# Two-layer cross-attention on one core: the layer-1 unit's second LayerNorm pass, its gamma pass and its beta pass move later in the turn

## What is computed

```python
def layer(emb, latent, Wq, bq, Wk, bk, Wv, bv, gamma, beta):
    q = emb @ Wq + bq                       # 224 x 512
    k = latent @ Wk + bk                    # 750 x 512
    v = latent @ Wv + bv
    w = softmax((q @ k.T) / sqrt(512), axis=query rows)
    x = w @ v + emb
    mu, var = mean(x, -1), var(x, -1)
    return (x - mu) * rsqrt(var + 1e-6) * gamma + beta
out = layer(layer(x, ctx, L0 weights), ctx, L1 weights)
```

## Time and profile before

| | us |
|---|---|
| median of 3 runs | 1000.95 (1000.65 to 1000.99) |
| the profiled execution, its own time | 1000.18 |
| its span, first to last instruction | 998.4 |
| TensorE busy | 975.7 (98%) |
| VectorE busy | 859.5 (86%) |
| ScalarE busy | 760.2 (76%) |
| GpSimd busy | 766.1 (77%) |
| TensorE's granted clock, mean | 0.998 of full speed |

### The profile page before, as it was taken

How to read it: one execution, slowest core, us unless ns; L and a number is a source line. 1 busy time by engine, 2 the same in 40 slices (tenths; PEclk the granted TensorE clock), 3 DMA queues, 4 the chain that set the end, 5 groups by cost and what they waited for, 6 DMA issues and landing times.

```text
span 998.4 us, 25754 instructions
## 1 busy us (share of the span) xinstructions
PE 975.7 (98%) x7300; PEld 910.6 (91%) x7300; DVE 859.5 (86%) x2602; ACT 760.2 (76%) x2128; POOL 766.1 (77%) x709
## 2 busy tenths in 40 slices
PE   7999999999999999999999999999999999999997
PEld 6889999999999999999999999999999999999986
DVE  5888988988888988888888888898888898888867
ACT  3667887777887777887777787777788777788764
POOL 0437788887888787878778878787878878888884
PEclk9999999999999999999999999999999999999999
DMA  7754443554344454343455344455444455434101
GB/s 207 178 104 103 98 102 89 106 116 98 82 101 97 95 112 99 82 104 94 93 112 104 83 99 100 86 112 106 85 99 97 86 112 111 94 91 103 37 17 50
DMA packets 358998, 98.37 MB, mean 99 GB/s; under 512 B 308648, under 2 KB 342821, under 8 KB 358949
## 3 DMA queue, kind: packets, MB, share of 16 engines
q1 hardware_dynamic: 356405, 96.98, 43.8%
q10 hardware_dynamic: 2544, 0.80, 0.4%
HBM read 83.06 MB, written 14.68 MB: 98 GB/s over the span
## 4 chain that ended last, share of the span: by engine, by line
PE 90%; DVE 3%; SPq 2%; issue 2%; ACT 1%; POOL 1%; DMA 1%; DVEq 0%; ACTq 0%; POOLq 0%
PE oq_bank L787 9%; PE score_bank L743 9%; PE score_bank L748 8%; PE score_bank L744 8%; PE oq_bank L797 6%; PE pv_bank L834 6%; PE oq_bank L772 6%; PE pv_bank L836 6%; PE pv_bank L843 6%; PE oq_bank L720 5%; PE oq_bank L715 5%; PE oq_bank L716 5%; PE oq_bank L773 5%; PE t_bank L672 2%; PE oq_bank L810 1%
## 5 line engine op out<-in xcount | busy, mean ns | idle before, releaser
L1083 ACT ACTIVATE probs<-probs,neg_max 125x224 f32<-125x224 f32 x378 | 177.8, 473 | 94.2 <-DVE neg_max L1523 94.2
L743 PE MATMUL score_bank<-qT_hi,cT_hi 128*125 128x224 f32 x768 | 196.2, 282 | 5.9 <-issue 4.1
L744 PE MATMUL score_bank<-qT_hi,cT_lo 128*125 128x224 f32 x768 | 188.3, 272 | 0.0
L1927 POOL TENSOR_TENSOR p_lo<-probs,p_hi 125x672 fp32r<-125x672 f32 x60 | 98.3, 1638 | 84.6 <-DVE p_hi L1559 84.6
L1111 ACT ACTIVATE probs<-probs,rsum 125x224 f32<-125x224 f32 x378 | 153.7, 474 | 1.4 <-DVE rsum L1543 1.4
L743 PEld LDWEIGHTS score_bank<-qT_hi,cT_hi 128*125 128x125 f32 x768 | 144.7, 188 | 10.6 <-issue 9.3
L1523 DVE CUSTOM_DVE_ANT_0 probs<-score_bank,d_row 125x224 f32<-125x224 f32 x384 | 139.2, 382 | 10.2 <-PE score_bank L748 6.6
L748 PE MATMUL score_bank<-qT_lo,cT_hi 128*125 128x224 f32 x768 | 147.2, 273 | 0.7 <-DVE qT_lo L1506 0.7
L744 PEld LDWEIGHTS score_bank<-qT_hi,cT_lo 128*125 128x125 f32 x768 | 144.8, 189 | 0.0
L772 PE MATMUL oq_bank<-p_hi,raw_hi 125*128 125x224 f32 x480 | 140.6, 318 | 0.0
L715 PE MATMUL oq_bank<-xT_hi,A_hi 128*128 128x224 f32 x512 | 120.8, 275 | 0.3 <-ACT xT_hi L1055 0.2
(11 more groups left out here) (169 smaller groups left out, 2907.1 us busy)
## 6 DMA issues: line engine op xcount, KB each, us to landing
cb<-in_ctx_dram SPq DMA_DIRECT2D x248, 92.0 KB
raw<-in_ctx_dram SPq DMA_DIRECT2D x31, 500.0 KB
x<-in_x_dram SPq DMA_DIRECT2D x32, 448.0 KB, 4.0
xb<-in_x_dram SPq DMA_DIRECT2D x124, 112.0 KB, 2.7
out_dram<-y_out SPq DMA_DIRECT2D x31, 448.0 KB, 4.2
raw<-in_ctx_dram SPq DMA_DIRECT2D x62, 125.0 KB
cb<-in_ctx_dram SPq DMA_DIRECT2D x124, 3.5 KB
y<-in_L_xattn_Wq_dram SPq DMA_DIRECT2D x2, 512.0 KB, 5.4
```

Of the source, the lines that this page charges most:

```text
L743: nc.tensor.matmul(o, cT_hi[:, u.slot, l, cols], qT_hi[:, l, :], start=(l == 0), stop=False)
L744: nc.tensor.matmul(o, cT_lo[:, u.slot, l, cols], qT_hi[:, l, :], start=False, stop=False)
L1083: ins = act.activation(probs[0:MP, u.par4, c, :], probs[0:MP, u.par4, c, :], ACT.Exp, bias=neg_max[0:MP, u.par4, c:c + 1], scale=-1.0, acc ...
```

## The change

Three steps are moved, and nothing is added or removed. On ScalarE `standardise(b(-2), 1)` goes from right behind `standardise(b(-2), 0)` to behind the two `normalise(b(-1))`. On GpSimd `scale(b(-2), 1)` goes from the head of the turn to behind `sum_probs(b(-1))`, and `raw_lo_part(a(+0), 0)` now stands ahead of `add_beta(b(-2), 1)` instead of behind it.

```diff
@@ ScalarE, turn(i, j) @@
                 exps(b(-1), 0)
                 o_hi(a(-1), 1)
                 standardise(b(-2), 0)
-                standardise(b(-2), 1)
                 ctxT_hi(a(+0), 0)
                 exps(b(-1), 1)
                 q_hi(a(+0), 0)
                 normalise(b(-1), 0)
                 normalise(b(-1), 1)
+                standardise(b(-2), 1)
                 ctxT_hi(a(+0), 1)
                 q_hi(a(+0), 1)
@@ GpSimd, turn(i, j) @@
                 a, b = units(i, j)
-                scale(b(-2), 1)
                 add_beta(b(-2), 0)
                 probs_lo(b(-1))
                 last_probs_lo(b(-1))
@@
                 sum_two(b(-1))
                 sum_probs(b(-1))
+                scale(b(-2), 1)
+                raw_lo_part(a(+0), 0)
                 add_beta(b(-2), 1)
-                raw_lo_part(a(+0), 0)
                 scale(a(-1), 0)
                 scale(a(-1), 1)
                 probs_lo(a(+0))
```

## The result

| | before | after |
|---|---|---|
| median of the runs | 1000.8 us (4 runs) | 1014.14 us (4 runs, 1013.83 to 1014.62) |
| ratio to before | | 1.0135 [1.0117, 1.0152] |
| the profiled execution, its span | 1000.18, 998.4 us | 1014.15, 1012.3 us |

A forecast was written before the change was run, and what follows sets the result against it. It took the turn chain, through GpSimd's gamma passes holding VectorE's layer-1 dots, as the bound: 27 turns of 30.13 us add 11.0 us, the ends 0.7, giving 1011.9 profiled and 1012.6 us median; range 1000 to 1018.

The forecast's parts named there:

- The exponentials: ScalarE, layer-1 unit: without the standardise pass ahead of them they start at about 488.63 instead of 489.18, 0.55 us earlier.
- The two gamma passes: GpSimd, layer-0 unit: they begin at offset 18.35 to 18.40 instead of 17.06, on top of VectorE's two layer-1 dots.
- The handover: GpSimd and VectorE exclude each other: first dot from 19.45, second pass 20.06, second dot 21.15, VectorE free at 22.33.
- slower still: Rival: both layer-1 dots wait behind both gamma passes, 30.47 us a turn, 1022 us; chance 0.08.
- Every turn 30.13 us: All turns last about 30.13 us instead of alternating 30.03 and 29.61; 27 turns take 813.5 us against 802.5.
- The ends: The turn before and the one behind the 27 turns: 0.35 us added for each, 0.7 us.
- its wait in the layer-1 o product: TensorE: its last four matmuls there return to about 0.6 us; a wait appears in the layer-0 o product instead.
- Store and loads: Store 2.5 + 0.1 us later, context load packets end near 29.4, hidden by 0.4 us or more in the longer turn.
- no change: Rival: late context loads replace TensorE's wait for weights, 29.7 us a turn, 1000.4 us; chance 0.12.
- Faster: Rival: VectorE takes both dots at once, unheld, and the 0.55 us counts; 29.5 us a turn, 995 us; chance 0.13.
- The lock as the cause: GpSimd passes and VectorE's two-SBUF-input operations exclude each other on one port pair; argued from a held dot at 51.79.
- 11 us for handovers at the very end of an instruction: If the lock held for whole instructions, each of two handovers is 0.2 us later and the sum up to 11 us more.

The follow-up runs named there:

- experiment 7: Changed kernel with only SyncE's loads of the turned context issued ahead of the store; 1012.12 us, ratio 1.0115.
- experiment 5: Changed kernel with the second layer-0 gamma pass cut from 512 to 16 columns, so not the whole computation; 1001.38 us, ratio 1.0004.
- experiment 11: Kernel of experiment 10 with GpSimd's layer-1 beta pass add_beta(b(-2), 0) moved ahead of inverse_deviation(a(-1)); 994.73 us, ratio 0.9938.
- experiment 2: Changed kernel with ScalarE's order as before, so GpSimd's part of the change alone; 1011.07 us, ratio 1.0102.
- experiment 4: Changed kernel with add_beta(b(-2), 1) ahead of raw_lo_part(a(+0), 0), and scale(a(-1), 1) behind the wait for the layer-0 dots; 1009.85 us, ratio 1.0093.
- experiment 10: Changed kernel with GpSimd's passes placed clear of layer-1 dots and p_hi cast, and SyncE's loads ahead of the store; 997.22 us, ratio 0.9961.

## Why the prediction was right

Point by point, with the profile of after.

- **The exponentials** were to be 0.55 us earlier: 0.56.
- **The two gamma passes** were to start at 18.35 to 18.40: 18.30 to 18.39 in nearly all turns. The second one was to be recorded with about 1.9 us and took 1.7 to 1.8.
- **The handover.** Forecast: first dot from 19.45, second pass from 20.06, second dot from 21.15, VectorE free at 22.33. In the turn shown: 19.46 (512.76 less 0.75), and 21.16, free at 22.26. The first dots are recorded with 0.97 to 1.60 us, the second ones with 1.65 to 1.68; the forecast had about 1.35 and near 1.6. The handover went wrong in 2 of the 29 turns in which both passes meet the dots (first dot 2.23 and 2.63 us, turns of 30.62 and 30.44): that is the mechanism of "slower still", which so has its place, but rarely.
- **Every turn 30.13 us:** 30.02 to 30.12 in all but the few named (30.42, 30.62 and 30.44), mean 30.12; two lengths have become one. 27 turns took 813.2 us where 813.5 were forecast.
- **The ends** are the term that was mis-sized: 0.7 us given, 3.2 measured (14.0 us between the profiled executions, less 10.7 in the 27 turns). The turn ahead of the 27 is 31.04 us against 29.67, 1.4 us more, since its inverse sum moved from offset 21.87 to 23.26 with the held dots. The end takes 0.95 us more. The remaining 0.85 us lies ahead of that turn, which starts at 99.32 instead of 98.47. Of this, 0.66 us is there at the first turn_ctx of all (43.81 against 43.15), a place that lies anywhere from 43.07 to 44.10 in the fourteen kernels; in experiment 7, whose order on the compute engines is the same, the turn starts at 98.27. So it looks like a spread of the opening and not like the passes' doing, but one profile of each kernel doesn't show that. This, less the 0.3 us that the turns gave back, is why the times are above the forecast (the profiled one by 2.2 us, the median by 1.5).
- **TensorE** was to lose its wait in the layer-1 o product and get one in the layer-0 one. The second half came out, at the start of the product (L772, for qT_lo), not at its low-part matmuls. The first half came out in one kind of turn only: there the last four take 0.62 to 0.65 us. In the other kind, that of the turn at 492.55, they still take 0.75 us and 0.39 us of issue time follow, after 0.84 and 0.42. Why they do, with weights that are ready 0.6 us earlier, was not settled.
- **Store and loads** were to be hidden by 0.4 us or more. They landed 0.4 to 0.7 us ahead in most turns and 0.02 to 0.07 us ahead in three. The forecast had that at nothing; the trace shows one wait of 0.3 us, and experiment 7 sets the bound of 2 us. The 29.7 us a turn of the rival "no change" is what experiment 5 measured.
- **The rivals.** "Faster" at 995 was worked out at 29.5 us a turn; by experiment 5 the loads end at 29.7, so this rival would have been 1001. The kernel at 994.7 needed SyncE's order.
- **The lock as the cause** was argued from one event of the opening. Experiment 5 shows it by taking a pass's length away at that place, and experiment 11 by moving the passes: dots of 0.75 us again and a turn that is shorter than before. That 11 also has SyncE's new order; experiment 7 shows that this order alone leaves the dots held. The Trainium skill, "SBUF — State Buffer", section "SBUF: two separate sides", says that the loser fully blocks; the held dots here agree but for their last 0.2 us. The forecast's 11 us for handovers at the very end of an instruction was too low by its own numbers: the pass between the two dots would start 0.14 us later too, 0.54 us a turn in all, 15 us. The forecast's own sum took the 0.20 and 0.14 us of the earlier trace rows instead, and these are what the turn shows.

The step that a reader could have got wrong is the first one on GpSimd: it had 2.28 us of idle time behind its gamma passes, 77% busy, and looks free to take a pass. That idle time was the time of VectorE's dots.

## What to carry to other kernels

Before moving a pass onto an engine's idle time, look at what the other engine does in that idle time: idle time of GpSimd beside VectorE's SBUF operations may be what keeps these short, and here one pass of 1.3 us put ahead of it, which pushed another pass onto the dots, cost 10 us over the kernel by itself (experiment 2). A gain upstream is only worth something if every wait between it and the next turn has slack, so list the second and third bound (here loads at 29.7 us a turn behind dots at 30.1) and clear them together: SyncE's order alone was worth 2, 13 or 19 us, depending on what else was in the way. And a store that waits for compute should not stand ahead of loads that don't.

## What was not expected of the hardware

More than the dots is held by GpSimd's passes over SBUF: the cast of p_hi (0.50 us alone, 1.13 to 1.46 under a pass in experiment 4), and even the addition of epsilon to 112x2 elements. GpSimd's and VectorE's timeline of the kernel of experiment 5:

```profile
483.55 1.63 POOL L1962 TENSOR_TENSOR psum<-probs 125x672 f32<-125x672 f32 x1
484.31 0.90 DVE L1643 TENSOR_SCALAR ve<-mv 112x2 f32<-112x2 f32 x1
```

It takes 0.17 us when GpSimd is not in a pass, and here it ends at 485.21, so it began at 485.04, 0.14 us before the pass's end. The held end differs: a dot begins 0.20 us before the pass's shown end, the cast and this one 0.14 us.

GpSimd's short passes follow the same rule. The name psum in their rows is that of a tile in SBUF (`psum3 = sb("psum3", [P, HALF, T])`), which holds partial sums. In the kernel of experiment 10, GpSimd's timeline and VectorE's:

```profile
483.38 1.00 POOL L1970 TENSOR_TENSOR psum<-psum 125x224 f32<-125x224 f32 x1
484.46 1.00 POOL L1977 TENSOR_TENSOR psum<-psum 125x224 f32<-125x224 f32 x1
```

```profile
483.02 0.83 DVE L1496 CUSTOM_DVE_ANT_0 dot_junk<-x,w_row,c_col 112x512 f32<-112x512 f32 x1
483.89 1.03 DVE L1496 CUSTOM_DVE_ANT_0 dot_junk<-x,w_row,c_col 112x512 f32<-112x512 f32 x1
```

The sums take 0.67 us elsewhere and a dot 0.75. This looks as if the two slowed each other, but counted back from their ends they take turns. The first sum ends at 484.38, so it began at 483.71, 0.14 us before the first dot's end. The second dot ends at 484.92 and began at 484.17, 0.21 us before the end of that sum, and the second sum began at 484.79, 0.13 us before the end of that dot. Whether the waiting is at a port or in the way in which instructions are let in was not tried.
